# Keys scaled on GpSimd, a new order of stages, and TensorE's batches written out, in a fused attention block

## What is computed

```
xn = layernorm(x)
x  = x + attention(xn)          # 16 heads of 8, over all 512 tokens
       + six_layers(xn)
for each of 6 layers:
    x = attn_layer(shift_tokens(x)) + x
    x = ffn_layer(shift_tokens(x)) + x
attn_layer: q, k, v = split(x @ Wqkv)      # 16 heads of 64
    q = l2norm(q) * q_scale ; k = l2norm(k) * k_scale
    q = q*cos*scale + rotate_half(q)*sin*scale ; k likewise with 1/scale
    sim = q @ k.T * 8 in windows of 32 tokens, each with the window ahead of it, masked
    out = softmax(sim) @ v @ Wo
ffn_layer: layernorm, W1, a * gelu(gate), W2
```

## Time and profile before

| | |
|---|---|
| median of 3 runs | 3598.78 us (3591.31 to 3603.01) |
| the profiled execution | 3596.61 us |
| its span, first to last instruction | 3594.8 us |
| TensorE matmuls busy | 3418.6 us (95%) |
| VectorE busy | 3173.1 us (88%) |
| ScalarE busy | 2346.6 us (65%) |
| GpSimd busy | 1507.8 us (42%) |
| GpSimd additions (line 832), 384 | 904.7 us, mean 2368 ns |
| VectorE scalings (line 898), 384 | 459.4 us, mean 1218 ns |

### The profile page before, as it was taken

How to read it: one execution, slowest core, us unless ns; L and a number is a source line. 1 busy time by engine, 2 the same in 40 slices (tenths; PEclk the granted TensorE clock), 3 DMA queues, 4 the chain that set the end, 5 groups by cost and what they waited for, 6 DMA issues and landing times. The chain is left out here.

```text
span 3594.8 us, 150765 instructions
## 1 busy us (share of the span) xinstructions
PE 3418.6 (95%) x64800; PEld 1945.6 (54%) x64800; DVE 3173.1 (88%) x3696; ACT 2346.6 (65%) x3217; POOL 1507.8 (42%) x924
## 2 busy tenths in 40 slices
PE   5999969999999999999999999999999999999997
PEld 2333335555555555555555555555555555555554
DVE  6999958889899898899889899898998989999894
ACT  3888746665766667666676666767666676666764
POOL 3333234344444444444444444444444434444441
PEclk7999979999999999999999999999999999999999
DMA  2000011111111111111111111111111111111112
GB/s 73 2 1 1 1 44 38 32 42 31 35 52 37 42 31 43 36 48 39 31 47 32 36 51 32 47 31 37 52 37 39 31 47 32 47 39 32 47 31 68
DMA packets 59837, 132.38 MB, mean 37 GB/s; under 512 B 10420, under 2 KB 33464, under 8 KB 59320
## 3 DMA queue, kind: packets, MB, share of 16 engines
q1 hardware_dynamic: 59320, 124.04, 11.9%
HBM read 23.58 MB, written 4.19 MB: 8 GB/s over the span
## 5 line engine op out<-in xcount | busy, mean ns | idle before, releaser
L1103 PE MATMUL slot<-w_qkv,xs 128*128 (+1 forms) x2304 | 1096.9, 606 | 34.4 <-ACT xs L955 30.5
L832 POOL TENSOR_TENSOR cosq<-cosq,sinq 128x1024 f32<-128x1024 f32 x384 | 904.7, 2368 | 442.1 <-DVE sinq L872 436.3
L827 POOL TENSOR_TENSOR half_sq<-sq 128x1024 f32<-128x1024 f32 x192 | 453.9, 2364 | 1302.3 <-ACT sq L963 1290.4
L1103 PEld LDWEIGHTS slot<-w_qkv,xs 128*128 128x128 f32 x2304 | 405.3, 191 | 410.8 <-issue 397.2
L870 DVE TENSOR_TENSOR cosq<-slot,table 128x1024 f32<-128x1024 f32 x384 | 468.5, 1220 | 67.2 <-ACT sq L963 60.7
L963 ACT ACTIVATE sq<-slot 128x1024 f32<-128x1024 f32 x384 | 393.5, 1025 | 193.9 <-PE slot L1103 193.7
L872 DVE TENSOR_TENSOR sinq<-slot,table 128x1024 f32<-128x1024 f32 x384 | 466.5, 1215 | 0.0
L898 DVE TENSOR_TENSOR qk<-cosq,ry 128x1024 f32<-128x1024 f32 x384 | 459.4, 1218 | 1.3 <-POOL cosq L832 1.3
L1052 PE MATMUL slot<-ident,qk 128*128 128x128 f32 x3072 | 399.4, 276 | 33.4 <-issue 16.3
L1052 PEld LDWEIGHTS slot<-ident,qk 128*128 128x128 f32 x3072 | 350.1, 142 | 149.4 <-issue 82.3
L1126 PE MATMUL slot<-oT,w_o 128*128 128x512 f32 x768 | 342.4, 599 | 2.4 <-DVE oT L923 2.4
(11 more groups left out here) (120 smaller groups left out, 4684.0 us busy)
## 6 DMA issues: line engine op xcount, KB each, us to landing
vb<-va SPq DMA_DIRECT2D x192, 390.0 KB, 3.5
vb<-va SPq DMA_DIRECT2D x144, 130.0 KB, 3.7
w_qkv<-in_w_qkv SPq DMA_DIRECT2D x56, 192.0 KB, 3.0
w_o<-in_w_o SPq DMA_DIRECT2D x6, 512.0 KB, 5.0
w<-in_w SPq DMA_DIRECT2D x6, 342.0 KB, 5.0
res<-in_x SPq DMA_DIRECT2D x4, 512.0 KB, 6.1
out<-w_qkv SPq DMA_DIRECT2D x8, 256.0 KB, 3.1
kept<-res SPq DMA_DIRECT2D x1, 1536.0 KB, 8.4
```

The lines of the kernel that those rows point to most:

```text
L827: nc.gpsimd.tensor_tensor(half_sq[:, :, :], squares[:, :, 0, :], squares[:, :, 1, :], ALU.add).then_inc(S["folded"], 1)
L832: nc.gpsimd.tensor_tensor(cosq[:, side], cosq[:, side], sinq[:, side], ALU.add).then_inc(S["qk"[side] + "_added"], 1)
L1103: last = nc.tensor.matmul(slot(kind, n)[:, i, :], xs[:, n * P:(n + 1) * P], w_qkv[:, unit // BATCH % 2, "qkv".index(kind), i * SEQ:(i + 1) ...
```

## The change

The diff below leaves out only renamed arguments. It

- moves scale_k from VectorE to GpSimd, with the same operands and waits (the entry scale_k3 that is left in DVE_ORDER matches no branch of VectorE's stages and issues nothing);
- gives TensorE, VectorE, ScalarE and GpSimd new orders and deals the PSUM slots anew;
- writes TensorE's 48 batches out, each at an aligned address, in place of four batches and a loop;
- drops passed() ahead of s, va and vb on TensorE.

```
 PE_ORDER = stages(
-    "kT2- q3- h0-- qT2- h1-- r1- h2-- s2- v2- v3- vb1- va1- q0 r2- k0 qT3- va2- kT3- q1 s3- y-- vb2- r3- kT0 k1 "
-    "qT0 vb3- v0 va3- k2 q2 s0 wo- r0 qT1 kT1 vb0 va0 k3 centre- s1 var- v1 ")
+    "va0- var-- q3- s1- qT2- v2- kT2- v3- s2- r1- h0-- h1-- h2-- vb1- q0 va1- kT3- k0 qT3- r2- q1 va2- s3- y-- "
+    "vb2- k1 qT0 r3- kT0 vb3- v0 k2 va3- s0 q2 wo- r0 kT1 v1 vb0 qT1 k3 centre- ")
 DVE_ORDER = stages(
-    "turn2-- vb3-- va3-- rotate_k1- turn3-- norms1- s0- scale_q1- scale_k1- rotate_q2- residual-- rotate_k2- "
-    "norms2- va0- vb0- turn0- scale_k2- s1- z-- rotate_k3- scale_q2- rotate_q3- hid0-- norms3- hid1-- s2- hid2-- "
-    "scale_q3- scale_k3- va1- vb1- turn1- rotate_q0 rotate_k0 norms0 va2- s3- scale_k0 y-- vb2- scale_q0 "
-    "rotate_q1 ")
+    "scale_q3- hid1-- hid2-- vb1- va1- rotate_q0 turn1- rotate_k0 norms0 va2- s3- scale_q0 vb2- y-- turn2- "
+    "rotate_k1 rotate_q1 vb3- norms1 va3- turn3- s0 rotate_k2 scale_q1 norms2 rotate_q2 residual- vb0 scale_q2 "
+    "rotate_k3 scale_k3-- va0 z- rotate_q3 s1 norms3 s2 hid0- turn0 ")
 ACT_ORDER = stages(
-    "next- exp2- v3- square_q0 r2- square_k0 qT3- kT3- norm0 square_q1 exp3- r3- kT0 qT0 square_k1 v0 square_q2 "
-    "norm1 exp0 square_k2 r0 qT1 shift- norm2 kT1 square- square_k3 root- v1 affine- kT2 square_q3 exp1 qT2 "
-    "to_gelu- gate0- r1 gate1- gate2- to_exp- norm3 v2 ")
+    "square_q0 exp2- kT3- square_k0 r2- qT3- norm0 exp3- square_q1 square_k1 qT0 r3- kT0 square_k2 v0 norm1 "
+    "square_q2 exp0 norm2 r0 kT1 shift- qT1 square_k3 square- v1 root- square_q3 qT2 affine- v2 kT2 exp1 norm3 v3 "
+    "to_gelu- gate0- r1 next gate1- gate2- to_exp- ")
 POOL_ORDER = stages(
-    "add_q3-- fold0- add_k0- add_q0- add_q1- fold1- add_k1- fold2- add_q2- add_k2- fold3- add_k3- ")
+    "add_k1-- add_q1-- scale_k1-- fold2-- add_k2-- scale_k2-- add_q2-- fold3-- add_k3-- add_q3-- scale_k3-- "
+    "fold0- add_q0- add_k0- scale_k0- fold1- ")
...
 SLOTS_OF = (
-    "q3 h2 vb1 va2 y kT0 vb3 k2 va0 centre",
-    "qT2 r1 v3 k0 r3 qT0 va3 q2 qT1 k3",
-    "kT2 h1 v2 q0 kT3 s3 vb2 k1 wo kT1 s1",
-    "h0 s2 va1 r2 qT3 q1 v0 s0 r0 vb0 v1",)
+    "s1 s2 h2 kT3 q1 va3 wo k3",
+    "v2 r1 q0 r2 va2 vb2 qT0 kT0 k2 kT1 qT1 centre",
+    "va0 qT2 v3 h1 va1 qT3 y r3 vb3 s0 r0 vb0",
+    "q3 kT2 h0 vb1 k0 s3 k1 v0 q2 v1",)
...
             if order is PE_ORDER:
-                for first in range(RUN):
-                    step(first, 0, None, first, False)
-
-                eng.addr_align(FETCH)
-                with eng.Fori(1, DEPTH * BATCH // RUN) as i:
-                    for s in range(RUN):
-                        if s:
-                            eng.addr_align(FETCH)
-                        step(RUN * i + s, (RUN * i + s) // BATCH, None, RUN + s, True)
+                for first in range(DEPTH * BATCH):
+                    eng.addr_align(FETCH)
+                    step(first, first // BATCH, None, first, False)
...
+                elif kind == "scale_k":
+                    wait(pool, "k_added", unit, n)
+                    wait(pool, "rooted", unit, n)
+
+                    wait_tile(pool, "kT_filled", unit, n)
+                    nc.gpsimd.tensor_tensor(qk[:, 1], cosq[:, 1].rearrange("p h a d -> p h (a d)"),
+                                            ry[:, HEADS:2 * HEADS, None].broadcast_to([P, HEADS, DH]),
+                                            ALU.mult).then_inc(S["k_scaled"], 1)
```

More of the change, by code:

```diff
@@ L640 @@
 FETCH = 256
-RUN = 4
 WINDOWS = (0, 2, 1, 3)
@@ L819, in _, with stage @@
             credit(pool, S, EVENTS, "pool")
-            def stage(kind, t, unit, batch, before, starts, layer):
+            def stage(kind, n, unit, batch, before, starts, layer):
                 if kind == "fold":
                     for name in "qk":
-                        wait(pool, name + "_squared", unit, t)
-                    wait_tile(pool, "sumsq", unit, t)
+                        wait(pool, name + "_squared", unit, n)
+                    wait_tile(pool, "sumsq", unit, n)
                     squares = sq[:, :, :, :].rearrange("p a h (e d) -> p (a h) e d", e=2)
@@ L828, in stage @@
                                             ALU.add).then_inc(S["folded"], 1)
+                elif kind == "scale_k":
[5 more added lines that the diff above has]
+                                            ALU.mult).then_inc(S["k_scaled"], 1)
                 else:
                     side = ("add_q", "add_k").index(kind)
-                    wait(pool, "qk"[side] + "_read", unit, t)
+                    wait(pool, "qk"[side] + "_read", unit, n)
                     nc.gpsimd.tensor_tensor(cosq[:, side], cosq[:, side], sinq[:, side], ALU.add).then_inc(
@@ L890, in stage @@
                     nc.vector.reduce_sum(ss[:, :], half_sq[:, :, :], AX.X).then_inc(S["sumsq"], 1)
-                elif kind in ("scale_q", "scale_k"):
-                    side = ("scale_q", "scale_k").index(kind)
-                    name = "qk"[side]
-                    wait(dve, name + "_added", unit, n)
+                elif kind == "scale_q":
+                    wait(dve, "q_added", unit, n)
                     wait(dve, "rooted", unit, n)
-                    wait_tile(dve, name + "T_filled", unit, n)
-                    nc.vector.tensor_tensor(qk[:, side], cosq[:, side].rearrange("p h a d -> p h (a d)"),
-                                            ry[:, side * HEADS:(side + 1) * HEADS, None].broadcast_to([P, HEADS, DH]),
-                                            ALU.mult).then_inc(S[name + "_scaled"], 1)
+                    wait_tile(dve, "qT_filled", unit, n)
+                    nc.vector.tensor_tensor(qk[:, 0], cosq[:, 0].rearrange("p h a d -> p h (a d)"),
+                                            ry[:, 0:HEADS, None].broadcast_to([P, HEADS, DH]),
+                                            ALU.mult).then_inc(S["q_scaled"], 1)
                 elif kind == "s":
@@ L1110, in stage @@
                     wait(pe, "kT_read", unit, n)
-                    passed(pe)
                     last = scores(n)
```

2 lines of the change are left out of this document (1 added, 1 removed).

## The result

The changed kernel takes **3727.8 us** (median; 3712.6 to 3731.5) against 3598.6, 1.0353 times as long (95% interval 1.0339 to 1.0368). The forecast was 3562 with a range of 3542 to 3634, so the sign was wrong and the time lies 94 us outside the range.

The account below looks back on a forecast made before the run. TensorE, 98% busy, was taken to bound the kernel. Terms -15 - 8 - 17 + 1 + 3 = -36 us took the span from 3594.8 to 3559, forecast as a 3562 us median; range 3542 to 3634.

Parts of the forecast that it names:

- The loop written out: TensorE's 48 batches: eleven loop turns of 1.36 us go, -15 us; aligned early batches and loop entry, -8 us.
- What it removes: TensorE's loop turns with their "issue" gaps, -15 us, and the excess of the slow early batches, -8 of 10.1 us.
- Register work ... nothing: TensorE's register work for w_qkv's address and passed()'s semaphore steps lie beside running matmuls: no gain from them.
- The new order: TensorE's steady batch: waits of 1.06 us go, 0.5 and 0.2 come; 63.07 to 62.7, -17 us over 47 batches.
- kT0's wait for qT0's copy: TensorE's kT0 uses qT0's slot, freed only after ScalarE's square_k1 and copy: one new wait, +0.5 us a batch.
- Scaling of keys on GpSimd: Four products a batch move to GpSimd at 2.34 us each (1.2 to 4.7); length covered unless VectorE is held up.
- VectorE loses four instructions a batch ... that alone gives nothing: VectorE sheds four steps of 1.14 us but already idles 5.7 us of an undisturbed batch: no gain.
- The race: scale_q0 on VectorE against scale_k0 on GpSimd: whichever starts first holds up the other; starts 0.1 us apart, unresolved.
- VectorE is first, free: The likelier outcome for scale_q0 against scale_k0: scale_k0 ends 1.1 us later, still ahead of kT0, at no cost.
- Boundary and start: Layer boundary 1.1 to some 1.3 us, five times, +1 us; start with one more GpSimd wait and chained units, +3.
- straight-line code starves: Rival: code that runs only once stalls TensorE, 4.5 us in each of 46 batches, 3769 us; chance 0.02.
- Lost race: Rival: GpSimd starts scale_k0 first and delays VectorE's scale_q0; 1.5 us a batch, 3632 us (3615 to 3640); chance 0.28.

Follow-up runs that it names:

- the version with the branch: The changed kernel with max_nops=4 in its alignment: at most 4 padding NOPs executed, a branch over the rest; 3538.12 us, ratio 0.9841.

## Why the prediction was wrong, step by step

**The loop written out: the step that failed.** "In the change each batch is aligned" stood there only as a gain. Alignment is paid in instructions, anything from 0 to 255 at a place, and no term of the sum and no end of the range held them. The trace of before had the price on show: its slow second batch, 695.84 to 764.48 in the earlier trace rows, holds the row of 718.36 quoted above, a 3.32 us "issue" behind 81 NOPs. I had put that batch's excess down to "their code not aligned"; half of it was the aligning. The steady batches all have the same length, so the same number falls to each: the 50 that came cost 2.27 us beyond the cover of 1.3, and 128, the middle of what was possible, would by the same 0.071 us a NOP have cost some 7.8 (an estimate). This one term is 107.5 us of stops, 20 at the start, and most of the 43 through the clock. The term that was put down at -23 for the writing-out as a whole came out, with its padding, as a loss of well over 100.

**What it removes** was right, even small. No "issue" ahead of every fourth batch (15 us), and the first batches run at 62.26 in the version with the branch, as the later ones do: the 10.1 us that they had over 63.07 are all gone, where -8 was taken.

**"Register work ... nothing" was wrong as well**, on the other side. Written out in its old order the steady batch takes 62.39 in place of 63.07. The 0.57 us ahead of q0 in the earlier trace rows, labelled "<-ACT xs", is gone there, with ScalarE's order untouched. The queue's records show what had stood in it. ScalarE's xs ends at 2642.96, TensorE's wait for it is over at 2643.00, and then come three more semaphore and register instructions (2643.11, 2643.25, 2643.40) before q0's first weight load at 2643.54. Written out there is one, and q0 starts 0.10 us behind the end of xs (2668.90 to 2669.00) in place of 0.59. So the label named the last event rightly, but nearly all of the gap was TensorE's own instructions behind it. The whole difference of the batch, 0.68 x 47 = 32 us, is gain that I had given in part to the new order and in part to nothing. The kernel written out alone keeps passed(), so this is the register work; what passed() costs no run separates.

**The new order**: forecast -17, measured -12 to -18, right in size but made otherwise, so that the size was luck. In the steady batch it gives 62.40 - 62.27 = 0.13, not 0.36, some 6 us over the stack, since the 0.57 was not its to remove. The rest of the 18.9 us between the two spans lies at the start and at the layer boundaries (1 us each), in two stops in the old order's last scores (3.6), and in a last batch and an end that are 4 and 2.7 us shorter. kT0's wait for qT0's copy is there in every batch, 0.27 in place of the estimated 0.5.

**Scaling of keys on GpSimd**: 1.90 us undisturbed, 2.12 in the mean, within the ends of 1.2 to 4.7 and below the 2.34 taken. Its length is covered, as said. "VectorE loses four instructions a batch ... that alone gives nothing" no run tests in the old order; in the new one, with the four put back, the kernel is 153 us slower.

**The race**: "VectorE is first, free": right, and run in nearly every batch. Tile 0's two scalings in the version with the branch:

```profile
2237.86 1.22 DVE L897 TENSOR_TENSOR qk<-cosq,ry 128x1024 f32<-128x1024 f32 x1
2237.96 2.88 POOL L827 TENSOR_TENSOR qk<-cosq,ry 128x1024 f32<-128x1024 f32 x1
```

That is k0 + 10.04 for VectorE (k0 is at 2227.82) and k0 + 10.14 for GpSimd, against 10.2 to 10.3 and 10.1 in the prediction. In 42 of the 48 batches, in this trace and in the changed kernel's, VectorE begins 0.08 to 0.12 us ahead; its scaling takes its 1.22, and GpSimd's takes 2.86 to 2.89 in place of 1.90. One more, the first, has VectorE's long scaling ahead of it; in the other five GpSimd is 1.75 us ahead and neither is longer than 1.24 and 1.90. So the reverse that no row showed then is shown now: a GpSimd product waits for a VectorE scaling that started before it. All but one of VectorE's scalings are at 1.2 to 1.3 us. The race was won by 0.1 us, which the rows could not resolve; that it was won is in that measure luck, and the chance of 0.28 for losing it was not too high.

GpSimd's additions have become longer by the same thing, 2.476 us in the mean against 2.368 before: 48 of the 384, one in each batch, take 3.3 us in place of 2.36, and each of these begins while VectorE's scaling of a query runs, 0.16 us behind its start. No other addition begins so. With the keys on VectorE the same 48 are long (mean 2.48), so it is the new order that does it and not the new product. None of it reaches TensorE's waits.

**Boundary and start**: the boundary costs 1.80 us in place of 1.11, +3 for the five where +1 was forecast. The start, forecast at +3, is +0.1 without padding (565.95 against 565.87), +20 with it.

**The sum without the padding**: 3538.1 - 3594.3 = -56 against the -36 forecast. The 20 between are the steady batch, 62.27 in place of 62.7, 47 times, and so mostly the register work. So without the padding the forecast would have been too cautious, but with the right sign. Of the rivals, "straight-line code starves" (3769, chance 0.02) came nearest in time, for another reason: code that runs once does run without stops if its borders lie well, and the kernel without alignment shows that it starves if they don't (3722). In the changed kernel such stops are 15.8 us of the whole. "Lost race", which made up nearly all of the slower side's 0.29, did not happen.

## To carry to other kernels

Where code is aligned, count what the aligning inserts and ask what runs on that engine just ahead of it: 50 NOPs cost 2.3 us a batch in one place behind a small matmul group, at most 0.2 with 31 of them spread over a long group and 19 left, and nothing visible under a branch. When stages are reordered or a loop is written out, the borders of the code move too; an "issue" gap of the profile that nothing explains should be looked up in the queue's own records before it is given a cause. And half a microsecond put down to a releaser may be register and semaphore instructions of the waiting engine itself: look whether they stand in the gap. Where two engines get in each other's way, compare mean and median of an instruction on both: here VectorE's showed nothing and GpSimd's did.

## What the runs showed of the hardware

- A NOP of padding takes 0.071 to 0.074 us on TensorE's queue (50 in 3.57, 161 in 11.8), and a taken branch over it 0.29 us, with no stop at a batch's head behind it.
- TensorE's code comes in 16 KB transfers of about 1 us, one for 256 instructions (ten in a steady batch of 2560). All 262 stops inside scores, in five traces, end 1.16 to 1.60 us behind such a transfer. With the borders moved by 128 instructions, at the same number of instructions in a steady batch, the kernel is 218 us slower (3727.8 to 3945.5), and 101 such stops, most of 1.1 to 2.0 us, take 157 of them.
- GpSimd's product of 128x1024 f32 with a broadcast factor takes 1.90 us, its addition of two such tiles 2.36. Begun 0.1 to 0.2 us behind a VectorE scaling whose inputs lie in SBUF, they take 2.88 and 3.27, and VectorE's stays at 1.22.
- Behind 20 of the 45 stops of 2.27 us the granted clock was at 0.50 for 3.4 us; behind none of the 45 stops of 1.17 us was it, and in the version with the branch not once between the first and the last wo. Four projection matmuls took 3.37 us at 0.50 in place of 1.88.
